# Adapter products of a routed mixture-of-experts body: eight half-height matmuls become four full-height ones, and copies lay out their operands

## The reference, cut to what matters

```python
def _fused_linear(x, W, qa, qb, scale, w):
    out = x @ W.T
    a = jnp.einsum('th,krh->tkr', x, qa)
    b = jnp.einsum('tkr,khr->tkh', a, qb)
    mix = jnp.einsum('tkh,tk->th', b, w)
    return out + scale[None, :] * mix

def expert(muW, gW, gqa, gqb, gs, uW, uqa, uqb, us, dW, dqa, dqb, ds, w):
    xe = x + w @ muW.T
    gate = jax.nn.silu(_fused_linear(xe, gW, gqa, gqb, gs, w))
    up = _fused_linear(xe, uW, uqa, uqb, us, w)
    return _fused_linear(gate * up, dW, dqa, dqb, ds, w)
```

## Time and profile before

| what | value |
|---|---|
| time, median of 3 runs | 1695.51 us (1692.44 to 1696.01) |
| span of the profiled execution | 1685.8 us |
| PE busy | 1568.4 us, 93% |
| DVE busy | 1155.5 us, 69% |
| POOL busy | 737.8 us, 44% |
| ACT busy | 617.2 us, 37% |
| chain that ended last | PE 63%, DVE 18%, issue 5%, ACT 5%, POOL 4%, DMA 3% |

### The profile page before, as it was taken

The page is one execution under the profiler, slowest core; times in us unless marked ns, Lnnn a source line. Parts: engine busy times, 40 slices in busy tenths (PEclk is TensorE's granted clock), DMA queues, the critical chain, the costliest instruction groups (busy, mean ns, idle before and its releaser), DMA issues.

```text
span 1685.8 us, 19547 instructions
## 1 busy us (share of the span) xinstructions
PE 1568.4 (93%) x6856; PEld 1155.1 (69%) x6856; DVE 1155.5 (69%) x1634; ACT 617.2 (37%) x971; POOL 737.8 (44%) x537
## 2 busy tenths in 40 slices
PE   3787799798888999999999999999999999999999
PEld 2343377566666677777777777777777777777776
DVE  5798964788999867487888755778888553333333
ACT  5545443444454434443343244333433321111111
POOL 4488510489898801077777301376786000000000
PEclk8799999899999999999999999999999999999999
DMA  7688627688787664765667445587665456566552
GB/s 251 215 285 315 254 80 253 201 290 297 270 289 286 253 255 172 248 228 205 232 238 258 152 161 196 202 275 257 238 208 180 175 200 210 184 222 222 195 181 85
DMA packets 111473, 375.87 MB, mean 223 GB/s; under 512 B 20176, under 2 KB 45776, under 8 KB 94864
## 3 DMA queue, kind: packets, MB, share of 16 engines
q1 hardware_dynamic: 101904, 340.81, 57.8%
q10 hardware_dynamic: 9472, 33.82, 5.8%
HBM read 304.33 MB, written 70.25 MB: 222 GB/s over the span
## 4 chain that ended last, share of the span: by engine, by line
PE 63%; DVE 18%; issue 5%; ACT 5%; POOL 4%; DMA 3%; SPq 0%; ACTq 0%; DVEq 0%; POOLq 0%
PE b_g L735 14%; PE b_u L735 14%; PE b_u L826 7%; DVE ring L1493 4%; PE b_g L826 3%; PE b_q L781 3%; PE b_q L826 3%; PE b_g L799 2%; DVE ring L1499 2%; PE b_g L766 2%; DVE tt L1467 2%; POOL ring L1392 2%; PE b_g L759 1%; POOL yx L1401 1%; DVE z L1467 1%
## 5 line engine op out<-in xcount | busy, mean ns | idle before, releaser
L1392 POOL TENSOR_TENSOR ring<-du,rep 128x512 f32<-128x512 f32 x256 | 344.5, 1349 | 151.4 <-DVE du L1571 91.9
L735 PE MATMUL b_g<-xnb,gm 128*128 128x512 f32 (+1 forms) x1440 | 356.2, 396 | 0.9 <-DVE xnb L1470 0.9
L735 PE MATMUL b_u<-xnb,gm 128*128 128x512 f32 (+1 forms) x1440 | 349.1, 391 | 0.0
L1493 DVE TENSOR_TENSOR_SCAN ring<-b_a,ring 128x512 f32<-128x512 f32 x256 | 310.8, 1214 | 15.7 <-ACT b_a L964 8.4
L1401 POOL TENSOR_TENSOR yx<-yx,ring 128x512 f32<-128x512 f32 x192 | 261.8, 1364 | 130.4 <-DVE ring L1499 129.9
L735 PEld LDWEIGHTS b_g<-xnb,gm 128*128 128x128 f32 (+1 forms) x1440 | 252.1, 179 | 89.1 <-issue 24.6
L735 PEld LDWEIGHTS b_u<-xnb,gm 128*128 128x128 f32 (+1 forms) x1440 | 257.1, 179 | 71.1
L1467 DVE SCALAR_TENSOR_TENSOR tt<-tt,b_g 128x512 f32<-128x512 f32 (+1 forms) x120 | 82.1, 684 | 222.7 <-ACT tt L964 222.5
L964 ACT ACTIVATE b_a<-delta,a_neg 128x512 f32<-128x512 f32 x256 | 173.6, 681 | 113.9 <-DVE ring L1493 113.9
L964 ACT ACTIVATE tt<-b_g 128x512 f32<-128x512 f32 (+1 forms) x120 | 71.1, 593 | 316.7 <-PE b_u L766 286.3
L826 PE MATMUL b_u<-dwt,hhl 128*128 128x512 f32 (+1 forms) x720 | 185.4, 394 | 0.0
(11 more groups left out here) (254 smaller groups left out, 2120.2 us busy)
## 6 DMA issues: line engine op xcount, KB each, us to landing
gm<-scr_gm SPq DMA_DIRECT2D x64, 1024.0 KB, 6.8
dwt<-scr_dw SPq DMA_DIRECT2D x32, 1536.0 KB, 6.8
rep<-bc_d ACTq DMA_DIRECT2D x64, 512.0 KB, 5.8
gm<-scr_gm SPq DMA_DIRECT2D x32, 768.0 KB, 4.4
dqt<-scr_dq SPq DMA_DIRECT2D x25, 896.0 KB, 9.1
scr_gm<-gm SPq DMA_DIRECT2D x20, 1024.0 KB, 7.5
scr_dw<-dwt SPq DMA_DIRECT2D x10, 1536.0 KB, 6.2
qat<-scr_qa SPq DMA_DIRECT2D x25, 512.0 KB, 10.2
```

Source lines behind the costliest of these rows:

```text
L735: i = mm(out_b[0:IW[m], :], w, v, start=(n == 0), stop=(n == 11 and not is_routed(s)))
L1392: v.tensor_tensor(ring[:, T % NRING], du[:, T % 4, :], rep[:, N % NREP, 0], ALU.mult).then_inc(pool_dbu, 1)
L1493: v.tensor_tensor_scan(w, ba[T % 2][:], w, 0.0, ALU.mult, ALU.add).then_inc(dve_scan, 1)
```

## The change

`adapters` gets operands with all 128 rows. `qbx` has four planes of width I: plane 0 is the gate's hi part in both halves of the rows, plane 1 the up projection's hi part in both halves, plane 2 has the gate's lo part in rows 0 to 63 and the gate's mask rows in 64 to 127, and plane 3 the up mask rows in 0 to 63 and the up lo part in 64 to 127. `awt` has four planes to match: `a_g` is hi of the gate above its lo, `a_u` lo of the up projection above its hi, `aw_g` and `aw_u` hold hi in one half and the routing weights in the other. So hi·hi and hi·lo become one matmul, and lo·hi and the mask another: four matmuls for each chunk instead of eight.

ACT still rounds `aw` once (into `aw_h`) and DVE still subtracts once (now in place in `aw`). Transfers of SP (`aw_load`) then place the halves: two copies of `ws`, two broadcast copies of `aw_h` when ACT is done, and two copies of `aw` when DVE is done. PE waits for their landing (`dma_awt`, `dma_wst2`) where it waited for `dve_awl`. The mask tile is split: its part for `qa_mask` goes into `gqa`, its rows for `adapters` into `qbx` (`gq_load`, behind the last `adapters` of the body before, since there is one buffer now). `ws` becomes one buffer `wsm`. In batch 0 the raw `qb` is rounded in four half-height pieces instead of one instruction and subtracted in two, and stored in two; later it is loaded in four. The constants are loaded in four transfers instead of two.

```diff
             def load(kind, s):
                 free(sp, kind, s)
...
+                if kind == "qb":
+                    at = scr[kind][w_index(s)]
+                    both = at[:, 0:I].rearrange("(j p) i -> p j i", j=2)
+                    for rows in (slice(0, HALF), slice(HALF, P)):
+                        sp.dma_start(qbx[rows, 0:2].bitcast(F32), both).then_inc(dma_t[kind], 16)
+                    sp.dma_start(qbx[0:HALF, 2].bitcast(F32), at[0:HALF, I:2 * I]).then_inc(dma_t[kind], 16)
+                    sp.dma_start(qbx[HALF:P, 3].bitcast(F32), at[HALF:P, I:2 * I]).then_inc(dma_t[kind], 16)
+                    return
...
             def gq_load(s):
                 r = rho(s)
-                if r >= 2:
-                    sp.wait_ge(pe_gu, IC * (body_of(r - 2) + 1))
-                sp.wait_ge(dma_gqs, 16 * NF)
-                sp.dma_start(gqt[r % 2][:].bitcast(F32), scr_gq[r % NF]).then_inc(dma_gq[r % 2], 16)
+                if r >= 1:
+                    sp.wait_ge(pe_gu, IC * (body_of(r - 1) + 1))
+                sp.dma_start(qbx[HALF:P, 2].bitcast(F32), scr_gq[r % NF][HALF:P, 0:I]).then_inc(dma_gq, 16)
+                sp.dma_start(qbx[0:HALF, 3].bitcast(F32), scr_gq[r % NF][0:HALF, 0:I]).then_inc(dma_gq, 16)
...
+            def aw_load(s):
+                r, e = rho(s), s % NX - 2
+                wsrc = ws_d[e * NK:(e + 1) * NK].rearrange("k r l -> (k r) l")
+                if r >= 1:
+                    sp.wait_ge(pe_gu, IC * (body_of(r - 1) + 1))
+                sp.dma_start(aw_g[HALF:P].bitcast(F32), wsrc).then_inc(dma_wst2, 16)
+                sp.dma_start(aw_u[0:HALF].bitcast(F32), wsrc).then_inc(dma_wst2, 16)
+                sp.wait_ge(act_aw, r + 1)
+                for rows, g_ in ((slice(0, HALF), 0), (slice(HALF, P), 1)):
+                    sp.dma_start(awt[rows, g_:4:2].bitcast(F32),
+                                 aw_h[rows].bitcast(F32).unsqueeze(1).broadcast_to([HALF, 2, L])).then_inc(dma_awt, 16)
+                sp.wait_ge(dve_awl, r + 1)
+                sp.dma_start(a_g[HALF:P].bitcast(F32), aw[0:HALF]).then_inc(dma_awt, 16)
+                sp.dma_start(a_u[0:HALF].bitcast(F32), aw[HALF:P]).then_inc(dma_awt, 16)
...
                 elif i < NX - 1:
                     w_load(s + 1)
+                    gqa_load(s + 1)
+                    next_pieces(s + 1, ("qa", "gm0", "gm1", "gm2"))
                     gq_load(s + 1)
-                    next_pieces(s + 1, ("qa", "gm0", "gm1", "gm2", "qb"))
+                    next_pieces(s + 1, ("qb",))
+                    aw_load(s + 1)
...
                 if m == 0:
-                    pe.wait_ge(dma_gq[r % 2], 16 * (r // 2 + 1))
-                    pe.wait_ge(dma_ws[r % 2], 32 * (r // 2 + 1))
-                g = gqt[r % 2]
-                for j, out_b in ((0, bg[m]), (1, bu[m])):
-                    rows = slice(j * HALF, (j + 1) * HALF)
-                    mm(out_b[0:IW[m], :], g[rows, cols], ws[rows, r % 2], start=False, stop=False)
-                if m == 0:
+                    pe.wait_ge(dma_gq, 32 * (r + 1))
+                    pe.wait_ge(dma_wst2, 32 * (r + 1))
                     ready(pe, "qb", s)
-                    pe.wait_ge(dve_awl, r + 1)
-                for k, (hl_, v) in enumerate(((0, aw_h), (0, aw_l), (1, aw_h))):
-                    for j, out_b in ((0, bg[m]), (1, bu[m])):
-                        rows = slice(j * HALF, (j + 1) * HALF)
-                        i = mm(out_b[0:IW[m], :], qbt[rows, hl_, cols], v[rows, :], start=False, stop=(k == 2))
+                    pe.wait_ge(dma_awt, 64 * (r + 1))
+                for out_b, w, v in ((bg[m], 0, a_g), (bg[m], 2, aw_g), (bu[m], 1, a_u), (bu[m], 3, aw_u)):
+                    i = mm(out_b[0:IW[m], :], qbx[:, w, cols], v, start=False, stop=(w >= 2))
...
+                if kind == "qb":
+                    rounded(qbx[0:HALF, 0], src[0:HALF, 0:I])
+                    rounded(qbx[HALF:P, 1], src[HALF:P, 0:I])
+                    rounded(qbx[HALF:P, 0], src[0:HALF, 0:I])
+                    rounded(qbx[0:HALF, 1], src[HALF:P, 0:I]).then_inc(act_hi[slot_of[k]], 1)
+                    return
...
+                if kind == "qb":
+                    src = raw[slot_of[k]]
+                    lo(qbx[0:HALF, 2], src[0:HALF, 0:I], qbx[0:HALF, 0])
+                    lo(qbx[HALF:P, 3], src[HALF:P, 0:I], qbx[HALF:P, 1]).then_inc(lo_done[slot_of[k]], 1)
+                    return
...
             def aw_first(s):
                 r = rho(s)
                 dve.wait_ge(pe_qa, r + 1)
+                need(dve, dma_awt, 64 * r)
...
             def aw_low(s):
                 dve.wait_ge(act_aw, rho(s) + 1)
-                lo(aw_l, aw[:], aw_h).then_inc(dve_awl, 1)
+                lo(aw[:], aw[:], aw_h[:]).then_inc(dve_awl, 1)
```

More of the change, by code:

```diff
@@ L76, in gated_ssm_moe @@
         dwt, dqt = sb("dwt", [P, 2, RAW], F32R), sb("dqt", [P, 2, Q_D], F32R)
-        qat, qbt = sb("qat", [P, 2, HC * P], F32R), sb("qbt", [P, 2, I], F32R)
-        gqt = [sb("gqt%d" % k, [P, GQ], F32R) for k in range(2)]
-        tile_of = {"gm0": gm[0], "gm1": gm[1], "gm2": gm[2], "dw": dwt, "dq": dqt, "qa": qat, "qb": qbt}
+        qat = sb("qat", [P, 2, HC * P], F32R)
+        qbx, gqa = sb("qbx", [P, 4, I], F32R), sb("gqa", [P, P], F32R)
+        qbn = qbx[:, 0:2]
+        tile_of = {"gm0": gm[0], "gm1": gm[1], "gm2": gm[2], "dw": dwt, "dq": dqt, "qa": qat, "qb": qbn}
         width = {"gm0": PW[0], "gm1": PW[1], "gm2": PW[2], "dw": RAW, "dq": Q_D, "qa": HC * P, "qb": I}
@@ L110, in gated_ssm_moe @@
         xn_h, xn_l = xnb[:, 0], xnb[:, 1]
-        wr, ws = sb("wr", [P, 2, L]), sb("ws", [P, 2, L], F32R)
+        wr = sb("wr", [P, 2, L])
         aw, dawf = sb("aw", [P, L]), sb("dawf", [P, L])
         inv_f = dawf[0:NE, 0:NE]
-        awp = sb("awp", [P, 2, L], F32R)
-        aw_h, aw_l = awp[:, 0], awp[:, 1]
-        rnd, daw_s = sb("rnd", [P, L], F32R), sb("daw_s", [P, L], F32R)
+        awt, aw_h = sb("awt", [P, 4, L], F32R), sb("aw_h", [P, L], F32R)
+        a_g, a_u, aw_g, aw_u = awt[:, 0], awt[:, 1], awt[:, 2], awt[:, 3]
+        wsm = sb("wsm", [P, L], F32R)
+        daw_s = sb("daw_s", [P, L], F32R)
         tt = sb("tt", [P, 2, L])
@@ L147, in gated_ssm_moe @@
         wT = aw[0:NE, :]
-        ss = ws[:, 1]
+        ss = wsm[:]
         ctx_raw = ring[:, 0:2]
         hold = [dqt[:].rearrange("p a n -> p (a n)")[:, m * L:(m + 1) * L] for m in range(HC - 1)]
-        hold.append(qbt[:].rearrange("p a n -> p (a n)")[:, 0:L])
+        hold.append(qbx[:].rearrange("p a n -> p (a n)")[:, 0:L])
         ctx_h, ctx_l = hold[0:2], hold[2:4]
-        u_h, u_l = [aw_h, aw_l, daw_s[:], ws[:, 0]], hold
-        s_r, s_st = ring[:, 3].bitcast(F32R), aw_h
+        u_h, u_l = [a_g, a_u, daw_s[:], aw_g], hold
+        s_r, s_st = ring[:, 3].bitcast(F32R), a_g
+        gw = ring[:, 3, 0:HC * NE].rearrange("p (c n) -> p c n", c=HC)
+        inv_i = ring[0:NE, 3, HC * NE:HC * NE + NE].bitcast(I32)
+        gq_st = [a_u[:, 0:GQ], aw_u[:, 0:GQ]]
         bcs = zt[0:HALF, :]
@@ L210, in gated_ssm_moe @@
         dma_x, dma_mu, dma_mq, act_z0 = (sem(n) for n in ("dma_x", "dma_mu", "dma_mq", "act_z0"))
-        dma_stg, dma_gq, dma_wr, dma_ws = (
-            [sem(n + str(k)) for k in range(2)] for n in ("dma_stg", "dma_gq", "dma_wr", "dma_ws"))
+        dma_stg, dma_wr = ([sem(n + str(k)) for k in range(2)] for n in ("dma_stg", "dma_wr"))
+        dma_gq, dma_gqa, dma_ws, dma_awt, dma_wst2 = (
+            sem(n) for n in ("dma_gq", "dma_gqa", "dma_ws", "dma_awt", "dma_wst2"))
         dma_s0 = [sem("dma_s0_%d" % k) for k in range(4)]
@@ L320, in ready @@
             if from_scratch(s):
-                eng.wait_ge(dma_t[kind], 16 * loads(kind, s))
+                eng.wait_ge(dma_t[kind], loaded(kind) * loads(kind, s))
             elif s == 0:
@@ L439, in w_load @@
                 need(sp, dve_dawf, r - 1)
[L440 to L441 removed]
+                need(sp, pe_qa, r)
                 sp.wait_ge(dma_wst, 64 * (b + 1))
@@ L444, in w_load @@
                 wsrc = ws_d[e * NK:(e + 1) * NK].rearrange("k r l -> (k r) l")
-                for h in range(2):
-                    sp.dma_start(ws[h * HALF:(h + 1) * HALF, k].bitcast(F32), wsrc).then_inc(dma_ws[k], 16)
+                sp.dma_start(wsm[HALF:P].bitcast(F32), wsrc).then_inc(dma_ws, 16)
                 for h in range(2):
                     sp.dma_start(wr[h * HALF:(h + 1) * HALF, k], src).then_inc(dma_wr[k], 16)
+            def aw_load(s):
[12 more added lines that the diff above has]
+                sp.dma_start(a_u[0:HALF].bitcast(F32), aw[HALF:P]).then_inc(dma_awt, 16)
             def w_store(b):
@@ L454, in w_store @@
                 if b > 0:
-                    for k in range(2):
-                        sp.wait_ge(dma_ws[k], 32 * (NF // 2) * b)
+                    sp.wait_ge(dma_ws, 16 * NF * b)
                 else:
@@ L785, in qa_mask @@
                 r = rho(s)
```

(14 more changed lines are left out.)

76 lines of the change are left out of this document (47 added, 29 removed).

## The result

The changed kernel is slower: 1714.97, 1716.86 and 1721.08 us in three executions, against a median of 1693.97 us for the kernel before; the ratio on record is 1.0157 (95% interval 1.0135 to 1.018), some 27 us more (23 to 30; the plain difference of the two medians is 22.9). A fourth execution of 1964.58 us, with a granted clock of 0.743, is left out of these numbers. The forecast was 6.5 us less, 1689.0 us in a range of 1680 to 1702, so the time lies outside the range, above even rival D's 1714.

What follows compares the result with a forecast made beforehand. It took DVE to set the pace in batch 0's bodies and PE to bound batches 1 to 3. Gains of 25.1 us minus costs of 18.6 gave 6.5 us less, 1695.5 to 1689.0 us, range 1680 to 1702.

Steps and rivals of the forecast that it cites:

- rival D: At PE's adapters: the lateness is not of the height switch and stays, only costs are left, 1714 us; chance 0.05.
- the transfers ahead of the first routed bodies: Batches 1 to 3: copies land late for the first adapters, 1.5 us in batches 1 and 2, 0.3 in 3; 3.3 us.
- SP's queue in batch 0: Batch 0's other bodies: six waiting copies hold SP's stores and raw dw and dq loads; 1.5 us over the batch.
- The gain: PE's adapters: lateness at switches between matmul heights saved, 0.42 us a group; together 25.1 us, bounds 20 and 27.5.
- The rule on tiling: PE's adapters: the skill's Tiling Modes section says changing the mode drains the engine; by that 0.42 us a group goes away.
- The second subtraction: Batch 0, DVE: a second half-height subtraction of qb costs 1.5 us in each of six bodies, 9 us.
- Rival B: Batch 0: SP's hold makes raw dw late, ACT and DVE wait; 13.2 us for 1.5, 1701 us; chance 0.20.
- the first routed body of batch 0: There ACT waits for the raw qa; some 0.44 MB more transfers ahead lengthen it by 1.6 us (0 to 3).
- The constants: Ahead of the first work: four transfers mean two more issues of 0.49 us; 0.7 us (0 to 1.0).

Runs made afterwards that it cites:

- e4: Kernel before, plus only a wait in SP's queue in batch 0, ahead of the raw dw and dq loads, until the next body's aw_low is done: ratio 1.0061.
- e10: Kernel before with four full-height adapter matmuls in place of eight, nothing else, output not the reference's: ratio 0.9886, 19.3 us faster.
- e3: Kernel before with batch 0's qb made in pieces as in the changed kernel, four roundings and two subtractions of 64 rows: ratio 1.0077.
- e6: Kernel before with batch 0's qb subtraction in two halves of 64 rows, rounding in one piece as before: ratio 1.0069.
- e1: Changed kernel with batch 0's raw dw and dq loads (bodies 3 to 9) issued ahead of the six copies and their waits: ratio 1.0103, 1708.08 us.
- e9: Kernel of e5 with ACT issuing a batch's first rep loads behind its first tanh of the first routed body: ratio 1.012.
- e5: Kernel of e2 with SP holding the load of dq and all loads behind it until the copies have landed: ratio 1.0127.
- e2: Changed kernel with the six copies issued ahead of dq's load for the first routed body of each batch: ratio 1.0145, 1715.6 us.
- e8: Changed kernel with batch 0's routed bodies and the first routed body of batches 1 to 3 in the old half-height form: ratio 0.9909, 1676.79 us.

## Why the prediction was wrong, step by step

The forecast was 6.5 us less, and 26.6 us more were measured. Three terms of the sum make most of the difference: the transfers ahead of the first routed bodies (3.3 us counted, 15.7 us of waits), SP's queue in batch 0 (1.5 counted, 10.3 in e4) and the gain (25.1 counted, 19.3 in e10).

**The gain** was right in its mechanism and 6 us too large, just under its lower bound of 20. The prediction had 25.1 us; e10 measures 19.3 (15 to 23). By the trace of e10 most bodies that PE bounds gain 1.17 to 1.23 us (1.26 predicted; e = 7 gains 0.98, and one body 0.47), e = 3 keeps 0.2 in both batches as forecast, and batch 0 gains about 1. What was not counted: e = 4 loses 1.4 us in one of the two batches, since PE's longer wait ends at the lower clock. The same wait of 2.0 us of the changed kernel had the clock at 0.69 behind it in batch 1 and at 1.00 in batch 2 (windows of the changed kernel at those places):

```profile
899.50:905.00 5.50, 5.23 (x16) 4.15 (x17) 5.50 (x9) 2.94 (x5) 4.12 (x3) 0.69 0.48 106
1260.40:1265.00 4.60, 4.51 (x20) 3.71 (x21) 4.60 (x8) 2.23 (x4) 3.22 (x3) 1.00 0.42 99
```

**The rule on tiling.** The drain at a change of mode (the Trainium skill, "TensorEngine Tiling (Array Packing)", Tiling Modes) agrees with e10: without the half-height matmuls the lateness of 0.44 us a group is gone. That it is a drain, and not something else that goes with the switch between heights, no run here shows.

**The second subtraction** was sized well: 11 us predicted with ACT's roundings (9 without), 13 in e3, 11.7 on DVE alone in e6.

**The step that failed first is "SP's queue in the other bodies of batch 0".** I took 1.5 us, from dw's landing alone: "the load goes at 454.6", "1.5 us of margin". The wait alone costs 10 us (e4), removing it brings 9 (e1). Two things were left out. First, I let `aw_low` stand where it stood before, 37 us into the body; in the changed kernel it ends at 471.73, 40 us into its body. Second, and mainly, I asked who waits for dw, and not what stands behind dw and dq in the queue: the raw `qa` of the next body. The timelines of SP, DVE and ACT in the changed kernel at the body that begins at 431.49:

```profile
434.02 0.60 SPq L387 DMA_DIRECT2D raw<-in_rr  x1
...
471.05 0.68 DVE L1520 TENSOR_TENSOR aw<-aw,aw_h 128x512 f32<-128x512 f32 x1
...
474.89 0.45 SPq L387 DMA_DIRECT2D raw<-in_dd  x1
...
445.38 0.63 ACT L1007 ACTIVATE qat<-raw 128x512 fp32r<-128x512 f32 x1 [3.96 <-DMA raw<-in_rr]
```

dw's load goes 43.4 us into the body, where it went 26.8 us in before. The load of the raw `qa` goes 2.5 us into a body as ever, but behind two stores and two large loads that were just let go, and takes 11.3 us to land instead of 4.1. ACT waits for it, then DVE, then PE at `qa` (the 11.8 us above), so that `aw` comes later still and SP is held longer. The chain of the changed kernel shows the loop: from `aw_low` through SP's issues to a raw load (here that of `gm`, which goes 2.3 us after the one of `qa`) and back to ACT.

```profile
422.38 0.83 DVE aw L1520
...
423.22 0.49 SPq L490
...
423.75 0.69 SPq L491
...
427.64 1.23 SPq L387
...
436.36 11.46 DMA raw<-in_gu
...
447.85 0.99 ACT gm L1007
```

Rival B named the hold and priced it at 13 us, near what was measured, but by the wrong wait (dw; ACT waited for it once, 6.5 us), so its number is near by luck, and it had 0.20.

**The transfers ahead of the first routed bodies** failed by more: they were sized at 3.3 us for three batches, and PE waits 11.3 us in these three, 15.7 in all four. The `rep` loads that I named are one cause (e9), but the sum treated a copy that waits for nothing else as 2.4 us. In flight with it are SP's own loads, of gm, qb, masks and dq ahead and dw behind. Batch 3 has no `rep` loads; I gave it 0.3 us, and it waits 3.5, of which holding the loads behind took most away (e5). And in batch 0, where "the DVE pace hides it", PE waits 4.5 us and the body is 2.3 us longer. The wait is not the whole price, since PE starts again at the lower clock behind it; in batch 3 of the changed kernel:

```profile
1440.68 1.02 PE L809 MATMUL b_g<-awt,qbx 128*128 128x512 f32 x2 [3.50 <-DMA awt<-aw]
1441.49 1.05 PE L809 MATMUL b_u<-awt,qbx 128*128 128x512 f32 x2
```

Two adapter matmuls take 0.81 us from start to start here, where they took 0.46 above. The three bodies e = 0 of batches 1 to 3 are 41.9, 43.1 and 39.7 us long, and 37.7, 37.7 and 34.3 in e10, which has no copies: 14.9 us for the 3.3 of the sum.

**The other terms.** For the first routed body of batch 0, I forecast a longer wait for the raw `qa` and it fell, from 5.39 to 2.72 us, most likely as the body itself comes later. The constants can't be told: the first routed body starts anywhere from 285.0 to 295.5 us in the profiles of this study, at 291.1 in e3, whose prologue is that of the kernel before.

**The sum of the parts.** -19.3 (e10) + 13 (e3) + 10.3 (e4) + 15.7 (waits for `awt`) = +19.7 us, against 26.6 measured (23 to 30). Each part is uncertain by some 4 us, so the rest of 7 is hardly outside. The traces say by stage where it lies. The two spans differ by 27.1 us: 4.9 before the first routed body (285.4 and 290.3, within the spread just named, so not to be put down to the change), 26.9 in batch 0's routed bodies up to the start of batch 1 (623.1 and 654.9), and -4.7 behind it.

| stretch | before | changed | e3 | e4 | e10 |
|---|---|---|---|---|---|
| batch 0 from its second routed body on | 289.7 | 314.4 | 304.3 | 300.3 | 290.3 |
| from the start of batch 1 to the end | 1062.7 | 1058.0 | 1062.7 | 1062.6 | 1042.7 |

In batch 0 the split (14.5) and the hold (10.6) add up to 25.1 us, and the changed kernel loses 24.7: neither their meeting nor PE's clock of 0.91 has anything left to explain there. From batch 1 on the four matmuls alone gain 20.0 us, and the changed kernel 4.7: the 15.3 us between them are the 14.9 of the first routed bodies. These are single executions: one body of batch 0 differs by up to 3 us between the traces of the changed kernel and e2, which have the same list there, and the whole stretch by 0.4.

## What to carry to other kernels

When a wait is put into a queue that issues transfers, price all the transfers behind it that any engine waits for, into the next turn of the loop, and not just the first (here 10 us where the first alone gave 1.5). A copy between two steps of a chain costs its time to land under the traffic of that moment, here about three times the 2.3 us that it took in e9. And a gain in one stage need not be bought in the others: with the old form in batch 0, where PE was not the bound, and in the first routed bodies, where the copies come late (e8), the change is 15 us faster instead of 27 slower.

## What was not expected of the hardware

Two copies of 64x512 that land 2.2 to 2.4 us after their issue in e9 took 6.4 to 6.9 us in the changed kernel with 1.5 MB of `rep` loads and SP's loads in flight. Loads issued after a copy delay it too: holding them back took batch 3's wait from 4.2 us in e2 to 1.1 in e5 (2.2 in e9). And PE's clock after the same 2.0 us of waiting was at the lower level in one batch (0.69) and full in the next.
